# Attention, layer norm and a dense layer on one core: the first norm folded into the dense weights

## What is computed

```python
x = L0_attn_x                                            # (1, 2048, 128), float32
x = _layernorm(x + attention(x, W_qkv, W_o))             # rotary positions, causal softmax
w = quantize_int4(kernel)                                # (128, 128)
x = _layernorm(x + (x @ w + bias + (x @ a) @ b))
```

## Time and profile before

| | before |
|---|---|
| median of three runs | 441.87 us (441.48 to 441.90) |
| the profiled execution | 441.07 us |
| its span, first to last instruction | 439.3 us |
| mean granted clock of TensorE | 0.981 |
| instructions | 8480 |

### The profile page before, as it was taken

The page is one execution under the profiler, slowest core; times in us unless marked ns, Lnnn a source line. Parts: engine busy times, 40 slices in busy tenths (PEclk is TensorE's granted clock), DMA queues, the critical chain, the costliest instruction groups (busy, mean ns, idle before and its releaser), DMA issues.

```text
span 439.3 us, 8480 instructions
## 1 busy us (share of the span) xinstructions
PE 412.0 (94%) x3246; PEld 199.0 (45%) x3246; DVE 380.5 (87%) x491; ACT 313.5 (71%) x532; POOL 119.5 (27%) x188
## 2 busy tenths in 40 slices
PE   5989799999899999999999999999999999999983
PEld 2547434443345443455343543344454444445652
DVE  2878789999999999998999999999999976766875
ACT  2454775676865877786878697868787889986850
POOL 8979511202112111212101222011003002135553
PEclk9999789999999999999999999999999999999995
DMA  7522212210000000021200022200000000000101
GB/s 238 181 98 93 104 60 79 66 38 3 0 1 4 1 1 5 0 77 59 69 2 2 3 70 75 57 2 1 1 1 2 1 2 3 2 3 2 27 25 48
DMA packets 12200, 16.57 MB, mean 38 GB/s; under 512 B 2444, under 2 KB 7324, under 8 KB 12160
## 3 DMA queue, kind: packets, MB, share of 16 engines
q1 hardware_dynamic: 11072, 15.75, 11.3%
q0 software_dynamic: 1088, 0.28, 0.4%
HBM read 10.37 MB, written 5.24 MB: 36 GB/s over the span
## 4 chain that ended last, share of the span: by engine, by line
PE 78%; DVE 11%; ACT 6%; issue 3%; DMA 1%; POOL 1%; POOLq 0%; SPq 0%; DVEq 0%; ACTq 0%
PE ps L1264 28%; PE ps L1250 20%; PE ps L1205 16%; DVE pmax L1026 10%; ACT probs L949 5%; PE ps L1173 3%; PE ps L1273 2%; PE ps L1219 2%; PE ps L1215 1%; PE ps L1179 1%; PE ps L1292 1%; PE ps L1229 1%; DMA x_sb<-in_L_attn_x_dram 1%; PE ps L1296 1%; PE ps L1189 1%
## 5 line engine op out<-in xcount | busy, mean ns | idle before, releaser
L1026 DVE TENSOR_REDUCE pmax<-ps 128x2 f32<-128x1024 f32 (+3 forms) x273 | 319.9, 1217 | 34.8 <-PE ps L1205 19.6
L949 ACT ACTIVATE probs<-ps 128x512 f32<-128x512 f32 (+4 forms) x465 | 281.8, 675 | 80.8 <-PE ps L1250 78.1
L1250 PE MATMUL ps<-qS,kS 64*128 64x512 f32 (+3 forms) x664 | 148.3, 404 | 3.5 <-DVE pmax L1026 2.3
L1264 PE MATMUL ps<-probs,vP 128*9 128x512 f32 (+3 forms) x1328 | 145.8, 520 | 0.1
L1205 PE MATMUL ps<-kS,qS 64*128 64x512 f32 (+3 forms) x640 | 137.9, 415 | 8.4 <-ACT probs L949 2.6
L1250 PEld LDWEIGHTS ps<-qS,kS 64*128 64x128 f32 x664 | 75.4, 186 | 82.5 <-ACT probs L949 38.4
L1205 PEld LDWEIGHTS ps<-kS,qS 64*128 64x128 f32 x640 | 65.2, 186 | 69.0 <-DVE pmax L1026 33.1
L854 POOL TENSOR_SCALAR_AFFINE_SELECT probs<-probs 128x512 f32<-128x512 f32 x64 | 40.6, 639 | 117.3 <-ACT probs L949 117.2
L863 POOL DMA_DIRECT2D qS<-mrows x34 | 19.7, 581 | 153.3 <-DVE mrows L1046 153.3
L1264 PEld LDWEIGHTS ps<-probs,vP 128*9 128x9 f32 x1328 | 21.4, 88 | 43.4 <-issue 28.3
L1219 PEld LDWEIGHTS ps<-causal_x,ident_x 64*128 64x128 f32 x188 | 17.8, 186 | 0.0
(11 more groups left out here) (116 smaller groups left out, 200.4 us busy)
## 6 DMA issues: line engine op xcount, KB each, us to landing
qS<-q_parts SPq DMA_DIRECT2D x52, 64.0 KB
kS<-k_parts SPq DMA_DIRECT2D x52, 64.0 KB
cs<-rope_tables_dram SPq DMA_DIRECT2D x4, 512.0 KB, 6.8
q_parts<-qp SPq DMA_DIRECT2D x4, 512.0 KB, 2.8
k_parts<-kp SPq DMA_DIRECT2D x4, 512.0 KB, 2.8
x_sb<-in_L_attn_x_dram SPq DMA_DIRECT2D x4, 256.0 KB, 5.7
out_dram<-rot SPq DMA_DIRECT2D x2, 256.0 KB, 2.3
qS<-mrows POOLq DMA_DIRECT2D x30, 8.0 KB, 1.8
```

The source lines that it names most:

```text
L949: nc.scalar.activation(probs[:, J % PRING, heads[0]:heads[-1] + 1:3 - len(banks), lo:hi], src, ACT.Exp, scale=float(DK) ** -0.5).then_inc( ...
L1026: nc.vector.tensor_reduce(dst, src, AX.X, ALU.max).then_inc(unit_free, 1)
L1250: last = nc.tensor.matmul(ps[:, bank, at:at + w], kS[rows, b, j // TPC, hp, (j % TPC) * TOK:(j % TPC + 1) * TOK], qS[rows, b, c, hp, lo:hi ...
L1264: last = nc.tensor.matmul(bank_of(("PV", n, 0))[VW * h:VW * h + VC, lo:hi], vP[:, j, HG * g + h, :], probs[:, J % PRING, h, lo:hi], start= ...
```

## The change

With C = I - 1/128 for the centring matrix, the normed rows are r C root, where r are the rows before the norm and root is a scalar per row. So (normed rows) (W + I) + bias is root (r (C (W + I))) + bias. The change uses this: the rows before the norm are turned in step 4; the identity is added to the low-rank product in PSUM, so that `quantise` leaves W + I; a new event K multiplies by C on TensorE, and VectorE copies the result to `ffn_c`; step 5 multiplies by `ffn_c`; and VectorE multiplies each tile by its root and adds the bias in one instruction a tile (`scalar_tensor_tensor`), in place of one addition for all tiles. NORM 0 and BIAS are gone. GpSimd makes C from the identity at the start of `weight_scale`. The steps that remain keep their order in `TURNS`; K is put in between, two score sets and one maxima product after L. Constants of `Course` change with it, among them those for weight loads, entries, signals and the work of M, O and the steps.

```diff
-POST_STEPS = (("POST", 2), ("POST", 3), ("RSTD", 0), ("NORM", 0), ("POST", 4), ("POST", 5), ("RSTD", 1), ("NORM", 1))
+POST_STEPS = (("POST", 2), ("POST", 3), ("RSTD", 0), ("POST", 4), ("POST", 5), ("RSTD", 1), ("NORM", 1))
...
-    LOAD, COLUMN, GAP, ENTRY, EXIT = 0.1, 1 / 2400, 0.016, 0.115, 0.08
-    TO_ACT, TO_DVE, TO_PE = 0.29, 0.17, 0.13
+    LOAD, COLUMN, GAP, ENTRY, EXIT = 0.096, 1 / 2400, 0.007, 0.122, 0.082
+    TO_ACT, TO_DVE, TO_PE, ACT_TO_PE = 0.302, 0.181, 0.149, 0.18
+    DVE_FIX, ACT_FIX, M_WORK, O_WORK, PLACED, VFIX = 0.064, 0.05, 0.51, 0.49, 1.25, 0.079
...
-    "SAVSSASASVDASOSASASVSSASSAVSASVDAVSSSAVASASSVOSASVDAVSASSSASOSASSADVADVDDMLVSSASSVASSSAVASDASVSADVVASASSSSAASSSVDAVMDADV"
+    "SAVSSASASVDASOSASASVSSASSAVSASVDAVSSSAVASASSVOSASVDAVSASSSASOSASSADVADVDDMLVSSAKSSVASSSAVASDASVSADVVASASSSSAASSSVDAVMDAD"
...
-    "SSSScdSSOfcgcddVVaeVShcSSSSSbeVceSSSedVVViddeSSSSSSVfdVSieSeegdVSSSSOfeVhdVafgeVVObfcfagbgdfheefcgdgigifffgfegfggghfhg")
+    "ScdSSOecfcVVaeVSgcSSSSSbeVceSSSddVVVSSSSSSVedVSSdefdVSSSSOeeVgdVaffeVVObfcfagbggedfcgefffdgegfggfgg"
...
-            def post_bias(n):
-                (first, end), i = tiles(n), turn(n)[0]
-                pool.wait_ge(normed[n], normed_count(n, 0))
-                nc.gpsimd.tensor_tensor(x1b[i][:, first:end, :], x1[i][:, first:end, :], bias_sb[:, :].rearrange("p (a d) -> p a d", a=1)
-                                        .to_broadcast([128, end - first, D]), ALU.add).then_inc(pool_post[n], 1)
-
             def weight_scale():
+                pool.tensor_scalar(centre[:, :], ident[:, :], 1.0 / D, None, ALU.subtract).then_inc(centre_set, 1)
...
+                if k == 5:
+                    dve.wait_ge(pool_post[n], pool_count(0))
+                    for t in range(first, end):
+                        last = nc.vector.scalar_tensor_tensor(res2[i][:, t, :], bank_of(e)[:, t * TOK:(t + 1) * TOK], rstd[i][:, t:t + 1], bias_sb[:, :],
+                                                              ALU.mult, ALU.add)
+                    last.then_inc(unit_free, 1)
+                    released(dve, e)
                 if k in (3, 5):
-                    norm = 0 if k == 3 else 1
-                    added = x_sb[:, c * TPC + first:c * TPC + end, :] if k == 3 else x1b[i][:, first:end, :]
...
+            def centred():
+                e = ("K",)
+                dve.wait_ge(unit_done, UNIT[e])
+                nc.vector.tensor_copy(ffn_c[:, :], bank_of(e)[:, 0:D]).then_inc(unit_free, 1)
...
-                nc.tensor.matmul(bank_of(e)[:, 0:D], aT[:, :], b_sb[:, :], start=True, stop=True).then_inc(unit_done, 1)
+                nc.tensor.matmul(bank_of(e)[:, 0:D], aT[:, :], b_sb[:, :], start=True, stop=False)
+                nc.tensor.matmul(bank_of(e)[:, 0:D], ident[:, :], ident[:, :], start=False, stop=True).then_inc(unit_done, 1)
+
+            def centre_rows():
+                e = ("K",)
+                banks_taken(pe, e)
+                released(pe, ("L",))
+                pe.wait_ge(centre_set, 1)
+                nc.tensor.matmul(bank_of(e)[:, 0:D], centre[:, :], ffn_q[:, :], start=True, stop=True).then_inc(unit_done, 1)
...
                 if k == 4:
-                    pe.wait_ge(normed[n], normed_count(n, 0))
+                    released(pe, ("POST", n, 3))
                 if k == 5:
-                    released(pe, ("L",))
+                    released(pe, ("K",))
...
                     if k == 4:
-                        last = nc.tensor.transpose(to, x1[i][:, t, :], ident[:, :])
+                        last = nc.tensor.transpose(to, res[i][:, t, :], ident[:, :])
                     if k == 5:
-                        last = nc.tensor.matmul(to, x1T[i][:, cols], ffn_q[:, :], start=True, stop=True)
+                        last = nc.tensor.matmul(to, resT[i][:, cols], ffn_c[:, :], start=True, stop=True)
```

More of the change, by code:

```diff
@@ L260, in reduced @@
     def reduced(self, end, work):
-        self.dve = max(self.dve, end + self.TO_DVE) + work
+        self.dve = max(self.dve, end + self.TO_DVE, self.scaling) + work
+        self.scaling = 0.0
         self.give(self.dve + self.TO_PE, self.took)
@@ L339, in take @@
             self.values = self.values[1:]
-            end = self.whole(0.094 + 0.853 * left(n, j) / CH, ready)
+            end = self.whole(self.VFIX + 0.853 * left(n, j) / CH, ready)
             i = self.probs.index(FAR)
@@ L351, in take @@
             g, c, first, end = TASKS[e[0]]
-            self.aside(0.55 * (end - first) / TPC, 0.6, ready)
+            self.aside(0.55 * (end - first) / TPC, self.O_WORK, ready)
             if g == FINAL[c]:
@@ L355, in take @@
         elif kind == "L":
-            self.aside(0.1, 1.8, ready)
-        elif kind == "BIAS":
-            self.pool = max(self.pool, ready) + 0.2 + 0.5 * (TASKS[e[0]][3] - TASKS[e[0]][2]) / TPC
+            self.aside(0.2, 1.8, ready)
+            self.due += ((self.dve + self.TO_PE, "K"),)
+        elif kind == "K":
+            self.aside(0.25, 0.3, ready)
         elif kind in ("POST", "NORM", "RSTD"):
@@ L361, in take @@
             share = (TASKS[n][3] - TASKS[n][2]) / TPC
[L362 removed]
             if copied_by_act(event):
[L364 to L366 removed]
+                self.act = at = max(self.act, self.whole(0.55 * share, ready) + 0.25) + 0.05 + 0.43 * share
+                self.give(self.act + self.ACT_TO_PE, self.took)
@@ L379, in take @@
-            step = POST_STEPS.index((kind, k)) + 1
-            if step < len(POST_STEPS):
-                self.due += ((at + (0.25 if "RSTD" in (kind, POST_STEPS[step][0]) else self.TO_PE), POST_STEPS[step][0], n, POST_STEPS[step][1]),)
+                self.scaling = self.scaled[n] if k == 5 else 0.0
+                self.aside((0.55 if k in (2, 4) else 1.0) * share, {2: 0.05 + 0.53 * share, 3: 0.2 + 0.53 * share, 4: 0.05 + 0.53 * share,
+                                                                    5: 0.1 + 0.9 * share}[k], ready)
@@ new lines, in take @@
+                at = self.dve + self.TO_PE
+                self.dve += {3: 0.05 + 1.05 * share, 5: 0.05 + 1.05 * share}.get(k, 0.0)
+            elif kind == "NORM":
+                self.dve = max(self.dve, ready) + 0.1 + 1.0 * share
+                self.closed += (n,)
+            else:
+                self.pool = at = max(self.pool, ready) + 1.0
+            if kind == "POST" and k == 2:
+                self.due += ((at, "POST", n, 3),)
+            if kind == "POST" and k == 3:
+                self.due += ((self.dve + 0.25, "RSTD", n, 0), (at, "POST", n, 4))
@@ L382, in take @@
+            if kind == "RSTD":
+                self.scaled = self.scaled[:n] + (at + 0.2,) + self.scaled[n + 1:]
+            if kind == "POST" and k == 4:
+                self.due += ((at, "POST", n, 5),)
+            if kind == "POST" and k == 5:
+                self.due += ((self.dve + 0.25, "RSTD", n, 1),)
+            if kind == "RSTD" and k == 1:
+                self.due += ((at + 0.2, "NORM", n, 1),)
         else:
@@ L408, in schedule @@
     for turn in left_over:
-        course.take(course.offer(turn, int(next(left_over), 17) if turn in "abcdefghi" else None))
+        course.take(course.offer(turn, int(next(left_over), 17) if turn in "abcdefg" else None))
     assert course.a == len(course.A) and course.s == len(course.S) and course.v == len(course.V) and not course.due
@@ L462 @@
 DIAGONAL = {e[1:3]: i for i, e in enumerate(e for e in SCHEDULE if e[0] == "S" and e[3] == 0 and on_diagonal(*e[1:3]))}
-POSTS = [e[1] for e in SCHEDULE if e[0] == "NORM" and e[2] == 1]
+POSTS = [e[1] for e in SCHEDULE if e[0] == "NORM"]
 TASK_END = {n: steps(n) - 1 for n in range(len(TASKS))}
```

106 lines of the change are left out of this document (53 added, 53 removed).

## The result

| | before | after |
|---|---|---|
| median of the runs beside each other | 441.88 us (four) | 452.89 us (four) |
| the profiled execution | 441.07 us | 452.73 us |
| its span | 439.3 us | 451.0 us |
| mean granted clock of TensorE | 0.981 | 0.984 |
| instructions | 8480 | 8489 |

Three runs of after lie between 452.67 and 453.06 us, the fourth at 457.21.

A forecast was written before the change was run, and what follows sets the result against it. TensorE alone sets the time up to 424.4 us, then a chain of small dependent steps. Tail -2.6 and weights +0.7 sum to -1.9, so 441.87 becomes 440.0 us; range 437.0 to 442.9.

The forecast's parts named there:

- the planner's constants: Changed constants deal PSUM banks and place operand loads anew: taken as 0, bounds 3.0 us either way.
- Rival B: Between 100 and 340 us, newly dealt banks open eight more waits of 0.34 us: 443.0 us, chance 0.20.
- Each new wait shortens the one behind it: Argument against slower bank dealing, in TensorE's waits on banks between 100 and 340 us; no size of its own.
- Rival C: The new dealing of banks closes TensorE's waits: -3.0 us, 437.0 us, chance 0.12.
- D: Tail chain stays, four new instructions costing far over 1.4 us, or K stalls over a microsecond: 441.9 us, chance 0.06.
- The weights: Near 203 us, extra TensorE passes for identity and K plus one copy: +0.7 us, bounds +0.2 and +1.3.
- The wait of 0.1 us for VectorE's weights: Near 203 us, K waits for the end of the quantised weights, at most about 0.1 us.
- The cover: Removed norms and biases of tasks 12 to 14 save nothing, since TensorE is busy 64.31 of 64.40 us there.
- The tail: Dependent steps after 424.4 us: the last norm ends at 434.26 against 436.88, -2.6 us.
- the rule weighed there: VectorE's next instruction waits for an empty pipe: four new ones 1.24 us, saving about 0.2 smaller; prediction went against it.
- Rival A: In the tail TensorE's clock falls all the same, task 16's product 0.9 us behind VectorE: 440.9 us, chance 0.20.
- The last store behind it is the same: At the kernel's end, the store after the last norm takes as long as before: no change.

The follow-up runs named there:

- the second kernel: The changed kernel with the PSUM banks and the operand-load places of the kernel before (K in bank 2): 441.86 us, ratio 0.9990.

## Why the prediction was wrong, and where it was right

**The step that failed** is the one on the planner's constants: "I take 0, because the waits on banks now are many and short [...], so new ones replace old ones", with bounds of 3.0 us either way. The dealing alone cost 16.3 us in the kernel before (458.46 - 442.17), and taking it out of after gives back about 11.9 (452.89 - 441.04, which were not measured beside each other). Waits did not replace each other: 20 became 33, and 7.3 us became 15.2. The row was read the wrong way round. Few short waits were the mark of an order fitted to its dealing, and the same row could have said that a dealing at random meets more of them. The bounds took a share of the idle time that there was, which says nothing of the idle time that there could be.

**Rival B** had this mechanism and a price some four times too small: eight waits more at 0.34 us. There were thirteen more, each longer on average (15.2 / 33 = 0.46 us), and what B left out, the clock fell behind two pairs of the new ones, near 88 and 108 us, where the lag grows by 6.4 us together. "Each new wait shortens the one behind it" held nowhere for long: up to 400 us the lag has hardly a step back. Rival C went the wrong way. D did not happen: the change does what it says. 

**The weights**: +0.7 was forecast with 1.3 as the upper bound. With the old banks it is 1.6 us at the place and 1.3 at the end. Of that, 0.55 is K's wait for the bank that it was given there; where nothing waits, L's passes cost 0.43 and K's 0.53 by the lag, so 0.96 where 0.7 was forecast. The wait of 0.1 us for VectorE's weights, which is part of the 0.7, is not seen. In after itself the price can't be told apart well: the lag grows 1.20 us there, but 0.79 over the same stretch in the kernel before with the new banks, 0.4 less.

**The cover** for the norms and biases of tasks 12 to 14 held: from 360 to 438 us TensorE is busy 77.94 of 78.00.

**The tail**: -2.6 forecast, -2.68 measured, and by the forecast's steps. Task 15's transposes follow step 3 directly, task 14's last norm is what VectorE does in place of NORM of task 15, and it, not TensorE, sets the next step. Four new instructions took 1.13 us (1.10 forecast), two 0.61 and 0.59 (0.58). That also bears on the rule weighed there: by the prediction's estimate from the rule of the Trainium skill, "VectorE: DVE Perf Modes", section "The DRAIN you can't avoid", that the next instruction waits until the pipe is empty, four of them would have taken 1.24; the row of the norms was the better guide. The prediction left out that the same section lets an instruction that is not held start earlier; the 1.13 us fit that.

**Rival A** fell: the clock was 1.00 from 438 to 443.6 us, and both products of step 5 took 0.68 where before had 1.19. The longest stop of TensorE there is 0.59. The Trainium skill, "TensorE: Matmul & The Clock Gate", section "What's actually happening", has the slow clock as the default and activity as what releases it; the trace agrees in that the clock stayed at 1.00 over these shorter stops.

**"The last store behind it is the same"** was wrong by 0.66 us. Without the dealing, the terms measured are 1.02 - 2.68 + 0.66 = -1.0 us (the second kernel's span, 438.3 against 439.3), where -1.9 was forecast. That span is of the fastest of its ten runs; the medians of the two kernels with the old banks do not tell a gain from none (0.9986 and 0.9990, both intervals with 1 in them), so of the -1.9 the traces show about half and the times nothing clear.

## What to carry to other kernels

When an order is written by hand and buffers are dealt by a program from constants, a change of a constant is a change of the kernel: compare which event holds which buffer, and how long after its last reader each is taken again, before costing anything at nothing. Time a change of constants alone, apart from the change that came with it. Here a loss of about twelve microseconds hid what the fold itself does: about one gained in the trace, too little for the medians, and 1.4 to 1.8 in the medians once K and the last store were seen to. A bound drawn from the waits that a fitted kernel has is no bound for those that it would have if the fit were lost.

## What the runs showed of the hardware

**An instruction fetch can hold up a store.** In the six traces in which an instruction packet falls into the last store, the longest landing is 2.6 to 2.9 us, in the six others the last store lands in 1.8 or 1.9; four VectorE instructions of almost no work moved the packet by 2.3 us and took the delay back. That the packet is VectorE's is inferred from this. It counts because the span ends with that store.

**The clock fell behind stops that are each under a microsecond.** Near 88 us of after, two stops of 0.84 and 0.81 us, 1.8 us apart from start to start of the work behind them, were followed by a granted clock of 0.50 for some 7 us, and stops of 0.85 and 0.98 us by one of 0.50 for 3.4 us from 109.2. At the first place in the changed kernel with the old banks TensorE is busy 1.92 and 1.83 of 2 us and its clock stays 1.00. All three traces with the banks of after have a low clock near both places, and none of the nine others has, so the dealing caused this too. In the tail of after, single stops of 0.55 and 0.51 us left it at 1.00. The length of the stops alone does not decide it: in before, stops of 0.69 and 0.64 us lie around the fall of the clock at 50.3 us, and in after stops of 0.69, 0.63 and 0.48 at the same place left it at 1.00.
